# Attention output offsets added by one-row products on TensorE, instead of two GpSimd sums per tile

## The reference, cut to what matters

```python
x = x + _L0_attn_ref(_layernorm(x), Wq, Wkv, Wo, bo, rel_emb)       # ... return out @ Wo + bo
x = x + _L0_xattn_ref(_layernorm(x), ctx, Wq, Wk, Wv, Wo, bo)       # ... return out @ Wo + bo
x = x + _L0_ffn_ref(_layernorm(x), ...)                             # router of 8 experts, best 2
```

## Time and profile before

| what | value |
|---|---|
| median of 3 runs | 2049.24 us |
| the three runs | 2055.61, 2049.24, 2044.33 us |
| the profiled execution, its own time | 2053.66 us |
| its span, first to last instruction | 2051.9 us |
| mean granted TensorE clock | 0.959 |
| TensorE matmuls busy, share of the span | 91% |
| GpSimd busy, share of the span | 47% |
| rounds 1 to 8, joined(1) to the last scatter | 912.08 to about 1033 us of the span |

### The profile page before, as it was taken

One profiled execution on the slowest core, in us unless ns is written; L12 is line 12 of the kernel. 1 busy time (PEld: TensorE's weight loads), 2 busy tenths in 40 slices (PEclk: granted clock), 3 DMA queues, 4 the chain that ended last, 5 costly groups with the idle time before them and its releaser, 6 DMA issues.

```text
span 2051.9 us, 52537 instructions
## 1 busy us (share of the span) xinstructions
PE 1871.6 (91%) x21476; PEld 1552.1 (76%) x21476; DVE 1301.8 (63%) x2932; ACT 973.9 (47%) x1984; POOL 967.1 (47%) x783
## 2 busy tenths in 40 slices
PE   7999999999999999987559489999999999988994
PEld 5677777777777777765447389999899999987873
DVE  6667676767676766647756565555565554556883
ACT  3666666666666666533136043334343443335451
POOL 2555555555555555545633733334234334435440
PEclk9999999999999999999869699999999999999996
DMA  6101020101230100234133520000220000220000
GB/s 246 50 19 47 19 78 19 50 19 70 101 129 19 50 12 12 70 133 130 47 135 126 155 78 13 23 13 13 79 80 26 19 18 18 85 73 16 15 14 16
DMA packets 74606, 119.85 MB, mean 58 GB/s; under 512 B 8392, under 2 KB 64464, under 8 KB 70992
## 3 DMA queue, kind: packets, MB, share of 16 engines
q1 hardware_dynamic: 69392, 105.31, 15.3%
q0 software_dynamic: 2560, 6.30, 1.1%
q10 hardware_dynamic: 2416, 4.88, 0.6%
HBM read 76.61 MB, written 39.85 MB: 57 GB/s over the span
## 4 chain that ended last, share of the span: by engine, by line
PE 41%; DVE 5%; POOL 3%; issue 2%; DMA 2%; ACT 2%; SPq 1%; POOLq 0%; DVEq 0%; ACTq 0%
PE psum L265 12%; PE psum L276 9%; PE psum L2019 4%; PE psum L2007 2%; PE psum L2511 2%; PE psum L1993 2%; PE psum L225 1%; PE psum L2545 1%; PE psum L1367 1%; PE psum L1350 1%; POOL b_yg L1484 1%; PE psum L246 1%; ACT e_pr L2650 1%; PE psum L1260 1%; PE psum L2520 1%
## 5 line engine op out<-in xcount | busy, mean ns | idle before, releaser
L774 POOL TENSOR_TENSOR a_sm<-a_sm,a_rsum 128x1024 f32<-128x1024 f32 x256 | 479.8, 1893 | 357.5 <-DVE a_rsum L808 355.1
L796 DVE CUSTOM_DVE_ANT_0 a_sm<-psum,a_strip 128x1024 f32<-128x1024 f32 x256 | 312.0, 1219 | 146.8 <-PE psum L628 146.8
L709 ACT ACTIVATE a_sm<-a_sm,a_mn 128x1024 f32<-128x1024 f32 x256 | 293.9, 1148 | 28.2 <-DVE a_mn L796 26.9
L714 ACT ACTIVATE a_pT<-psum 128x512 f32<-128x512 f32 x256 | 151.5, 592 | 273.1 <-PE psum L641 273.1
L641 PE MATMUL psum<-ident,a_sm 128*128 128x128 f32 x2048 | 275.2, 277 | 5.2 <-POOL a_sm L774 4.2
L641 PEld LDWEIGHTS psum<-ident,a_sm 128*128 128x128 f32 x2048 | 223.8, 140 | 62.7 <-issue 46.0
L656 PE MATMUL psum<-a_pT,a_V 128*64 128x256 f32 x2048 | 249.0, 385 | 0.6 <-ACT a_o L720 0.6
L656 PEld LDWEIGHTS psum<-a_pT,a_V 128*64 128x64 f32 x2048 | 136.1, 136 | 77.3 <-issue 22.1
L803 DVE COPY a_pT<-psum 128x512 f32<-128x512 f32 x256 | 174.8, 683 | 12.1 <-PE psum L641 4.9
L2103 ACT ACTIVATE g_val<-psum 128x512 f32<-128x512 f32 x64 | 38.0, 596 | 225.0 <-PE psum L2019 225.0
L628 PE MATMUL psum<-a_KH,a_QH 64*128 64x512 f32 x512 | 114.8, 445 | 2.5 <-DVE a_mn L796 2.5
(11 more groups left out here) (396 smaller groups left out, 3736.2 us busy)
## 6 DMA issues: line engine op xcount, KB each, us to landing
a_strip<-table SPq DMA_DIRECT2D x16, 960.0 KB, 6.7
oT<-a_o SPq DMA_DIRECT2D x64, 128.0 KB, 1.9
xs<-b_zeros SPq DMA_DIRECT2D x8, 1024.0 KB, 4.1
b_oT_in<-oT SPq DMA_DIRECT2D x7, 1024.0 KB, 5.9
y<-b_yb SPq DMA_DIRECT2D x23, 256.0 KB, 2.2
b_xs<-xs SPq DMA_DIRECT2D x23, 128.0 KB, 2.2
a_raw<-in_a_wqkv SPq DMA_DIRECT2D x7, 384.0 KB, 3.3
s_x<-in_x_rev SPq DMA_DIRECT2D x4, 512.0 KB, 8.0
```

Source lines behind the costliest of these rows:

```text
L709: a.activation(sm[:, st % RING, :], sm[:, st % RING, :], ACT.Exp, scale=-1.0, bias=mn[:, at:at + 1], accum_out=rsum[:, at:at + 1]).then_in ...
L714: a.activation(probs(st, 0), psum[:, 4, :].rearrange("p (k q) -> p k q", k=4), ACT.Copy).then_inc(sig("pT_act"), 1)
L774: g.tensor_tensor(sm[:, st % RING, :], sm[:, st % RING, :], rsum[:, at:at + 1].broadcast_to([P, T]), ALU.mult).then_inc(sig("scaled"), 1)
L796: v.tensor_tensor_reduce(out=sm[:, st % RING, :], in0=scores_banks(hl).rearrange("p c n -> p (c n)"), in1=strip[:, pair % 2, hl, qt * P:qt ...
```

## The change

TensorE gets a row of 128 ones, `one`, which GpSimd fills once. The last product of each block of ay and ay_rest is now followed by a product of this row (one row, 128 columns) with `bo_a` (one row, 256 columns), into the same PSUM area, and the same is done with `bo_b` after each product of by, except for tile 0. GpSimd's sums with `bo_a` and `bo_b` are gone; joined waits for the loaded rows itself, and crossed waits for `x1_bo` only at tile 0. TensorE waits before ay for the offsets and for the row of ones. The row takes 512 bytes of each partition, and what is allocated behind it moves by as much.

```diff
+    one = sb("one", [P, P])
...
         def attended(s, t):
             bank = banks("ay", s)
             for k in range(HP):
-                last = pe.matmul(bank[:, t * D:(t + 1) * D], (early["next"] if s == 1 else slots[s % 3])[0][:, k, t * P:(t + 1) * P], wo[:, k, :],
-                                 start=k == 0, stop=k == HP - 1)
-            return last
+                pe.matmul(bank[:, t * D:(t + 1) * D], (early["next"] if s == 1 else slots[s % 3])[0][:, k, t * P:(t + 1) * P], wo[:, k, :],
+                          start=k == 0, stop=False)
+            return pe.matmul(bank[:, t * D:(t + 1) * D], one[0:1, :], bo_a[0:1, :], start=False, stop=True)
...
                 pe.wait_ge(have("wo"), 16)
+                pe.wait_ge(have("bias"), 32)
+                pe.wait_ge(sig("filled"), 1)
...
                 for t in range(PT):
-                    last = pe.matmul(bank[:, t * D:(t + 1) * D], pT[:, t * P:(t + 1) * P], wvals[s % 3][:, :], start=True, stop=True)
+                    last = pe.matmul(bank[:, t * D:(t + 1) * D], pT[:, t * P:(t + 1) * P], wvals[s % 3][:, :], start=True, stop=not s)
+                    if s:
+                        last = pe.matmul(bank[:, t * D:(t + 1) * D], one[0:1, :], bo_b[0:1, :], start=False, stop=True)
...
-        def first_sum(s):
-            loaded(g, s)
-            g.tensor_tensor(slots[s % 3][1][:, :, :], slots[s % 3][1][:, :, :], over_tiles(bo_a[:, :], PT), ALU.add).then_inc(sig("x_bo"), 1)
-
...
+        g.memset(one[0:1, :], 1.0).then_inc(sig("filled"), 1)
         g.memset(ones[:, :], 1.0).then_inc(sig("filled"), 1)
...
-        first_sum(1)
...
-            if s + 1 < NP:
-                first_sum(s + 1)
-            if s < NP:
-                g.wait_ge(sig("bn_h"), PT * (s + 1))
-                g.tensor_tensor(x1[s % 2][:, :, :], x1[s % 2][:, :, :], over_tiles(bo_b[:, :], PT), ALU.add).then_inc(sig("x1_bo"), 1)
...
         def joined(s):
-            v.wait_ge(sig("x_bo"), s + 1)
+            loaded(v, s)
             v.wait_ge(sig("ay_ps"), s + 1)
...
         def crossed(s):
-            v.wait_ge(sig("x1_bo"), s + 1)
+            if s == 0:
+                v.wait_ge(sig("x1_bo"), 1)
             v.wait_ge(sig("by_ps"), s + 1)
```

More of the change, by code:

```diff
@@ L1311, in routing @@
                 pe.wait_ge(sig("m_mask"), s + 1)
-                pe.wait_ge(sig("filled"), 5)
+                pe.wait_ge(sig("filled"), 6)
                 if s:
@@ L1496, in gpsimd @@
         g.iota(turn_i[:, :], [[1, NU]], base=0, channel_multiplier=0).then_inc(sig("filled"), 1)
-        g.wait_ge(sig("filled"), 3)
+        g.wait_ge(sig("filled"), 4)
         g.affine_select(below[:, :], ones[:, :], [[1, P]], ALU.is_gt, 0.0, base=0, channel_multiplier=-1).then_inc(sig("filled"), 1)
@@ L1712, in vector @@
         v.tensor_scalar(limit[:, :], eight[:, :], float(CP), None, ALU.mult).then_inc(sig("made"), 1)
-        v.wait_ge(sig("filled"), 5)
+        v.wait_ge(sig("filled"), 6)
         v.tensor_copy(turn[:, :], turn_i[:, :]).then_inc(sig("made"), 1)
```

## The result

The changed kernel takes **2081.7 us** (median of four runs, 2071.32 to 2083.75). Its ratio to the kernel before, measured with it (2047.94 us, 2044.33 to 2055.61), is 1.0148 [1.012, 1.0177]: some 30 us slower, where 2049.6 and no change had been forecast. The profiled run took 2083.75 us.

A forecast was written before the change was run, and what follows sets the result against it. The prediction took each round as one loop through several engines, none full. Round 2 +1.4, rounds 3 to 6 -4.8 and rounds 7 and 8 +3.8 gave +0.4 us, so 2049.6 us against the 2049.24 median, range 2042 to 2058.

The forecast's parts named there:

- the price of a one-row product: On TensorE, each added product was put at 0.46 us, with bounds of nothing and 1.02 us.
- This takes for granted that ay stays at the full clock: Assumption for rounds 3 to 6, since TensorE idles about 1 us ahead of ay, less than round 2's 2.28 us.
- Slower, 0.05: the clock falls in most heads and ay_rests: Rival, chance 0.05: each further fallen stretch costs 1.69 us; +10.2 us needs six beyond the forecast.
- Rounds 0 and 1 hidden: Two added products in each, 0.9 us a round, disappear behind TensorE's waits for loads at the next heads.
- Round 2, +1.4: Three added products before crossed, 1.39 us, make joined(3) later by 1.4 us.
- Steady rounds, 14.91: Rounds 3 to 6 take 14.91 us each over crossed (round 4: 15.09), together -4.8 us.
- TensorE's way 0.2 us behind: In rounds 3 to 6 TensorE's own way takes 14.7 us, so VectorE's way sets the round by only 0.2 us.
- The 0.55 us feared from the indirect DMA alone: VectorE's gap might still be held up to 0.55 us without GpSimd's sums; the forecast sum would not change.
- Rounds 7 and 8, +3.8: Two products added before by_ps in each round, at the lower clock, cost 1.9 us a round.
- Rival 2: Chance 0.15: the clock stays up in rounds 7 and 8, making the sum -3.4 us.
- Rival 3: Chance 0.12: the clock falls at the heads of rounds 4 and 5 as before, 1.69 us each, sum +3.8 us.
- Rival 4: Chance 0.06: one-row products are nearly free, a gain down to -10.3 us.

The follow-up runs named there:

- e5: Changed kernel with the added products at 64 rows (of 1/64) instead of one row; 2069.75 us, ratio 1.0077 to the kernel before.
- e1: Changed kernel with the 28 added products at all 128 rows (of 1/128), same places; 2051.05 us, ratio 1.0005 to the kernel before.
- e10: Changed kernel with bo_a's one-row product leading each block of ay and ay_rest instead of ending it; 2076.58 us, ratio 1.0098.
- e2: Changed kernel without the 28 products, so neither offset is added for tiles 1 to 7; 2044.56 us, ratio 0.9965.
- e3: Changed kernel with one-row products for bo_a only, bo_b's sum given back to GpSimd; 2049.85 us, ratio 0.9997.
- e4: Changed kernel with one-row products for bo_b only, bo_a's sum given back to GpSimd; 2059.93 us, ratio 1.004.
- e7: Changed kernel with one-row products moved: bo_a's two behind mT, bo_b's as one of 512 columns ahead of the wait for bp_out; 2042.78 us, ratio 0.995.
- e8: Changed kernel with the added products at e7's places, but with all 128 rows; 2039.61 us, ratio 0.9936 to the kernel before.
- e12: e8 once more, in more executions against the kernel before; 2045.65 us, ratio 0.9956.
- e6: Changed kernel with each added product made twice, all 128 rows at half the value, 56 products; 2063.53 us, ratio 1.0055.
- e11: Changed kernel with 128-row products at the change's places, TensorE waiting for itself before and behind each; 2073.54 us, ratio 1.0074.
- e9: Changed kernel with by's two one-row products replaced by one of 512 columns ahead of the full ones; 2067.59 us, ratio 1.0053.

## Why the prediction was wrong, and where it was right

Two steps failed: the price of a one-row product, and the clock taken for granted. **The first** is the price of a one-row product, "I take 0.46 us, because the moving columns are as many as before". The nearest row was taken for the load's own duration (185 and 190 ns), which does hold: 182 ns with one row. What that mean hides is the neighbourhood: most of those loads of 64 rows stand among others of 64 rows. The trace of the kernel before had the change of rows too, where such a group begins and ends (weight loads of its attention stage):

```profile
601.41 0.19 PEld L628 LDWEIGHTS psum<-a_KH,a_QH 64*128 64x128 f32 x2 [0.38 <-issue]
601.52 0.19 PEld L628 LDWEIGHTS psum<-a_KH,a_QL 64*128 64x128 f32 x2
...
602.99 0.86 PEld L641 LDWEIGHTS psum<-ident,a_sm 128*128 128x128 f32 x8 [0.36 <-issue]
```

The load side idles for 0.38 and 0.36 us there, as it does for 0.33 at the added products: the trace before held a row for the cost of such a change, and the prediction did not use it. Between full products a one-row one costs 0.72 us behind the head, as shown above, and in by (2.48 - 0.93) / 2 = 0.78, since the full product behind it pays as well; behind ay_rest nothing follows at once, and it is 0.62. Put into the prediction's own steady round, 12.02 + 0.82 + 0.05 + 0.72 + 0.62 + 2 x 0.78 = 15.8 us; e5's round 5 measured 15.96, and e1, with 0.43 each, 14.78 against the 14.91 predicted.

The Trainium skill (TensorE: Matmul & The Clock Gate, "Why this matters for your kernels") gives a matmul of 32 rows the time of one of 128. No run here shows such a matmul alone. Among others it does not hold: 0.62 us with 1 or 64 rows between full ones, 0.43 with 128. The measurement decides; the sum "by that rule" was e1's, not this kernel's.

**The second, and the larger,** is the sentence "This takes for granted that ay stays at the full clock". The heads did (3.69 us in round 3), but by, bs and most of ay_rest fell. Of the 5.7 us between round 4 of the changed kernel and steady e1, 1.2 are the changes of rows at full clock (e5, round 5), and some 4.6 the clock. They can be read off one by one: by 4.56 - 2.48 = 2.1, bs 2.05 instead of about 1, ay_rest 5.29 - 3.70 = 1.6. The rival "Slower, 0.05: the clock falls in most heads and ay_rests" came nearest: one-row products do bring the clock down. But the heads stayed at the full clock, e10 shows that the end of a block is not the reason, and while its price, 1.69 us a stretch, fits ay_rest, it left out by and bs and so needed six stretches for 10 us. The argument against it, that the clock was 1.00 over rounds 2 and 3 with more idling, was about idling, and TensorE idled less than before, not more: it was busy for 18 of 20.5 us at the lower clock, and with the same products at the full clock for 13.55 of 15.96 us (e5, round 5), against 10.54 of 14.93 before.

Point by point:
- *Rounds 0 and 1 hidden:* right in rounds (10.81 for 10.70). joined(1) came 3.1 us later after ay(1), not 0.9: two products at 0.72, and 1.7 by a first block partly at the lower clock.
- *Round 2, +1.4:* wrong sign in e1, which took 13.59 for 14.91, since the head of round 2, ay(3), had waited 2.28 us for its load and did not any more. In the changed kernel +4.7, by the clock.
- *Steady rounds, 14.91, and rounds 4 and 5 without their losses:* right for full rows (e1: 14.78, 14.94, 14.78, 14.76), and "at nothing" right too (13.52; e2: 13.48, 13.64, 13.47, 13.47). The dependency picture held, the product's price did not.
- *TensorE's way 0.2 us behind:* right and decisive. With dearer products joined waits for TensorE in the rounds that lose, released by L1263 (10.7 us of idle VectorE in five rounds, beside 9.4 at joined(1)), so an added tenth is paid nearly in full.
- *gap:* never over 0.16 us in the changed kernel or in any experiment. The Trainium skill (SBUF — State Buffer, "Who interferes with whom") has a GpSimd instruction that reads SBUF and a VectorE instruction with two SBUF inputs shut each other out; the trace before agrees (gap ended with the second sum). The experiments with one sum a round back in place (e3, e4) do not test it, since gap never met a sum there. The 0.55 us feared from the indirect DMA alone did not come: in round 4 of e3 gap began at 963.75, inside a DMA from 963.05 to 964.01, and took 0.16 us.
- *Rounds 7 and 8, +3.8:* +4.8 in J7 to C7; e1, with full rows, had 23.04 for 20.04, +3.0.
- *Rival 2 (clock up in rounds 7 and 8):* no, 0.57 there. *Rival 3 (heads fall again):* no. *Rival 4 (one-row products nearly free):* no; even where TensorE waits anyway they cost 0.5 us a round (e7). Only full ones were free there (e8, e12).

In sum: predicted +0.4. With full rows J1 to C7 gave -4.1, ay(1) to joined(1) +2.5, and the medians +1, so that even there the sum came near by luck in part: 1.7 of the 2.5 us was the first block at the lower clock, and round 2 gained instead of losing. With one row it is +24.1 in J1 to C7 and +3.1 ahead of it.

**Theories.** "One-row products are dear only where they stand behind ay" fell with e10. "TensorE's longer way idles or stretches into a low clock" fell with e6. "The stall at each change of rows starves the clock" fell with e11, which stalls more. What is left, and what e1 against the changed kernel and e5 shows, is that in these rounds products of other row counts between full ones bring the granted clock down. Of rounds 2 to 6 all five fell in the changed kernel, four in e10, three in e5, three in e3, e4 and e9, which have fewer such products or changes, and one in e7, which has them elsewhere; none fell in e1, e2, e6, e8, e11 and e12. It is no rule for every place. In the attention stage of the kernel before, two changes of rows in every 6.3 to 6.8 us, with twelve records of 64 rows between them, leave the clock at 1.00 where TensorE has no idle time at all:

```profile
560.00:640.00 80.00, 80.00 (x638) 59.14 (x635) 55.81 (x115) 52.53 (x97) 46.88 (x26) 1.00 0.27 93
```

What stays open is why: no run here tells the change of rows from the rows that stand idle, at equal stall, nor how much TensorE's idle time ahead of by (0.69 and 0.79 us) has to do with it, nor why e5's rounds 2 and 5 stayed at 1.00 with the same instructions as rounds 3 and 4.

## What to carry to other kernels

An offset added on TensorE by a product with a row of ones should use all 128 rows (a block of 1/128 and the offset in every row), when its neighbours do: here that alone was worth some 30 us. Put such products where the engine already waits, as the opening of an accumulation ahead of a wait: in rounds 3 to 6 here they then cost nothing. When a change leans on a margin of tenths on the engine it loads, price the operation in its neighbourhood, from a row with the same neighbours (here, where a group of 64-row loads meets full ones), or call the price unknown in both directions.

## What was not expected of the hardware

- A weight load whose product has another row count than the one before waits for that product: 0.33 us of idle load side at the full clock, 0.65 at the lower; 0.62 and 1.14 us from start to start against 0.43.
- Four such products of two records each in a round of some 60 others bring the granted clock to 0.75 over a round in which TensorE is busy for 18 of 20.5 us (changed kernel, most rounds of e10, two of e5); four of 128 rows, or eight, or four with pauses of 0.75 us from start to start, leave it at 1.00.
- Behind the same idle time of 3.11 to 3.13 us the same block took 5.38 us in some kernels and 3.69 in others, so an idle time of that length can go either way.
